# Deferring the outer layer norm of each token half in a fused attention, FFN and MoE kernel

## What is computed

```python
def _L0_attn_ref(src, ...):                      # x is src
    attn = _sliding_attn(qkv, qkv, qkv, W)       # 16 heads of 64, window 256
    x = _layernorm(src + attn, ln1_g, ln1_b)
    ff = jnp.maximum(x @ W1 + b1, 0.0) @ W2 + b2 # 1024 -> 4096 -> 1024
    return _layernorm(x + ff, ln2_g, ln2_b)
x = L0_attn_src
x = _layernorm(x + _L0_attn_ref(x, ...), axis=-1)   # the "outer" layer norm
x = _layernorm(x + _L0_ffn_ref(x, ...), axis=-1)    # MoE: 8 experts, top 2
```

## Time and profile before

| | |
|---|---|
| median of the runs | 3103.24 us |
| lowest to highest of 3 runs | 3102.35 to 3196.35 us |
| the profiled execution | 3100.56 us |
| its span on the slowest core (core 3) | 3099.4 us |
| spans of the 8 cores in it | 3088.9 to 3099.4 us |
| busy on that core: TensorE, VectorE, ScalarE, GpSimd | 74%, 26%, 16%, 16% |

### The profile page before, as it was taken

How to read it: one execution, slowest core, us unless ns; L and a number is a source line. 1 busy time by engine, 2 the same in 40 slices (tenths; PEclk the granted TensorE clock), 3 DMA queues, 4 the chain that set the end, 5 groups by cost and what they waited for, 6 DMA issues and landing times.

```text
span 3099.4 us, 31648 instructions; the slowest of 8 cores (3088.9 to 3099.4 us)
## 1 busy us (share of the span) xinstructions
PE 2301.0 (74%) x11290; PEld 1085.2 (35%) x11290; DVE 796.2 (26%) x1503; ACT 507.9 (16%) x751; POOL 509.8 (16%) x604
## 2 busy tenths in 40 slices
PE   0477877622999089922289988999889998999874
PEld 0243434311444034411134433444344443444431
DVE  0022222266000520053323311333113321233233
ACT  0233333300310022000011111111111111111110
POOL 2477777500000000000000001000100001000000
PEclk9999999999999599965589999999999999999987
DMA  9300000100442244302022223222332223222242
GB/s 217 72 1 1 1 1 1 36 5 0 69 81 55 55 68 81 68 8 47 1 48 41 48 48 69 34 41 41 62 62 35 48 41 62 55 37 46 48 102 75
DMA packets 49832, 148.18 MB, mean 48 GB/s; under 512 B 4952, under 2 KB 7680, under 8 KB 47632
## 3 DMA queue, kind: packets, MB, share of 16 engines
q0 software_dynamic: 41888, 123.88, 23.0%
q1 hardware_dynamic: 7792, 22.27, 2.3%
HBM read 248.96 MB, written 8.42 MB: 83 GB/s over the span
## 4 chain that ended last, share of the span: by engine, by line
PE 69%; DVE 11%; issue 5%; DMA 5%; ACT 4%; SPq 3%; POOL 3%; DVEq 0%; ACTq 0%; POOLq 0%
PE ob L670 14%; PE hg L605 14%; PE hu L605 14%; PE hb L477 7%; PE hb L448 6%; PE ppv L282 5%; DVE x0s L131 4%; PE ps L340 3%; SPq L154 3%; DVE bn L131 3%; POOL strb L145 3%; ACT osb L141 2%; DMA x0s<-x 2%; DVE attnh L134 1%; PE ptm L302 1%
## 5 line engine op out<-in xcount | busy, mean ns | idle before, releaser
L605 PE MATMUL hg<-ubf,w1T 128*128 128x512 bf16 x2048 | 486.7, 381 | 18.5 <-DMA w1T<-w1tt 9.5
L605 PE MATMUL hu<-ubf,w1T 128*128 128x512 bf16 x2048 | 483.8, 379 | 0.0
L670 PE MATMUL ob<-a,w2t 128*128 128x512 bf16 x2048 | 460.2, 384 | 10.3 <-DVE a L131 9.1
L145 POOL TENSOR_TENSOR strb<-strb,msk 128x640 bf16<-128x640 bf16 (+4 forms) x320 | 358.9, 1150 | 200.6 <-ACT strb L141 173.0
L131 DVE TENSOR_TENSOR x0s<-pbf,x0s 128x1024 f32<-128x1024 bf16 x80 | 98.0, 1225 | 949.2 <-PE pbf L688 493.2
L605 PEld LDWEIGHTS hg<-ubf,w1T 128*128 128x128 bf16 x2048 | 200.5, 98 | 262.7 <-issue 24.6
L448 PE MATMUL hb<-ybf,w1buf 128*128 128x512 bf16 x1024 | 228.4, 386 | 83.7 <-DMA w1buf<-W1p 78.2
L670 PEld LDWEIGHTS ob<-a,w2t 128*128 128x128 bf16 x2048 | 199.6, 99 | 244.6 <-issue 22.8
L605 PEld LDWEIGHTS hu<-ubf,w1T 128*128 128x128 bf16 x2048 | 200.5, 98 | 241.9 <-issue 0.7
L141 ACT ACTIVATE sg<-hg 128x512 bf16<-128x512 f32 x256 | 152.8, 597 | 743.4 <-PE hu L605 743.4
L131 DVE TENSOR_TENSOR sg<-sg,crep 128x512 bf16<-128x512 bf16 x256 | 108.9, 426 | 597.3 <-ACT sg L141 574.2
(11 more groups left out here) (64 smaller groups left out, 894.4 us busy)
## 6 DMA issues: line engine op xcount, KB each, us to landing
w1T<-w1tt POOLq DMA_DIRECT2D x64, 512.0 KB, 5.2
w2t<-w2tt POOLq DMA_DIRECT2D x128, 256.0 KB, 4.6
w1buf<-W1p POOLq DMA_DIRECT2D x32, 512.0 KB, 5.2
w2buf<-W2p POOLq DMA_DIRECT2D x16, 1024.0 KB, 8.5
x0s<-x SPq DMA_DIRECT2D x1, 8192.0 KB, 51.5
x0s<-x POOLq DMA_DIRECT2D x2, 4096.0 KB, 24.6
out<-x0s SPq DMA_DIRECT2D x2, 4096.0 KB, 14.2
x0tm<-x0p POOLq DMA_DIRECT2D x20, 260.0 KB, 39.7
```

Of the source, the lines that this page charges most:

```text
L145: getattr(self.nc.gpsimd, name)(*args, **kw).then_inc(self.sGP, 1)
L605: ins = nc.tensor.matmul(hps[:], bass.AP(self.w1T, slot2 * 2048 + kc * 256 + hu * 128, [[2 * 2048, 128], [1, 128]]), self.ubf[:, kc, 512 * ...
L670: ins = nc.tensor.matmul(obp[:, 512 * nb:512 * nb + 512], self.w2t[:, dsl, eidx, 128 * jc:128 * jc + 128], self.a[:, eidx, jc, 1024 * half ...
```

## The change

The inner layer norm of a half stays where it was. What follows it (the wait on GpSimd's queue, the accumulating load, VectorE's wait for it and the outer layer norm) becomes a function, `outer_ln_half`. For half 0 it is called within half 1, after the last group of FF1 and ahead of the first `W2` load. For half 1 it is called after the barrier and the set-up of the MoE buffers, ahead of the build of `ubf`. That build is called four times for 4 tiles each, with a wait for the outer layer norm of the half in question, where it was called once for 16 tiles.

```diff
@@ phase_ffn
         for half in range(2):
             ... # FF1: 16 groups
                 prev_w1_user[gslot] = self.cT
+            if half == 1:
+                self.outer_ln_half(0)
             for dc in range(FC):
                 ... # FF2
             self.waitd("vector", self.mg_tok)
-            ln2m = self.layernorm(gb=2, tiles=range(8 * half, 8 * half + 8))
-            self.wait("gpsimd", self.sV, ln2m)
-            xr = self.gdma(
-                self.x0s[:, 8 * half:8 * half + 8, :],
-                bass.AP(self.x0.tensor, (Q0 + 1024 * half) * D,
-                        [[D, 128], [128 * D, 8], [1, D]]),
-                accum=True)
-            self.waitd("vector", xr)
-            self.layernorm(gb=None, tiles=range(8 * half, 8 * half + 8))
+            self.ln2m[half] = self.layernorm(gb=2, tiles=range(8 * half, 8 * half + 8))
+
+    def outer_ln_half(self, half):
+        self.wait("gpsimd", self.sV, self.ln2m[half])
+        xr = self.gdma(
+            self.x0s[:, 8 * half:8 * half + 8, :],
+            bass.AP(self.x0.tensor, (Q0 + 1024 * half) * D,
+                    [[D, 128], [128 * D, 8], [1, D]]),
+            accum=True)
+        self.waitd("vector", xr)
+        self.u1m[half] = self.layernorm(gb=None, tiles=range(8 * half, 8 * half + 8))
@@ build, after the barrier that ends the FFN
-            self.m_ubf = self.fm_build(self.ubf, self.obs[0])
+            self.outer_ln_half(1)
+            ubf_q = {}
+            for qd in range(4):
+                ubf_q[qd] = self.fm_build(
+                    self.ubf, self.obs[0], tiles=range(4 * qd, 4 * qd + 4),
+                    dep=self.u1m[qd // 2])
+            self.m_ubf = ubf_q[3]
             self.phase_gating()
```

More of the change, by code:

```diff
@@ L428, in phase_ffn @@
         prev_w2_user = {}
+        self.ln2m = {}
+        self.u1m = {}
         mig_g = 0
```

## The result

The changed kernel takes 3052.05 us in the median; the kernel before, beside it, 3102.99. The ratio of the two is 0.983, with a 95% interval from 0.9818 to 0.9841, so about 53 us are gained (49 to 56). That is 1.7%, under the 2% that the prediction took as measurable, but the interval lies clear of 1. The forecast was 3046 us and a gain of 57.

A forecast was written before the change was run, and what follows sets the result against it. TensorE was taken as held between the FFN halves by GpSimd's queue, then ScalarE's. Terms -70.1 + 15.4 + 1.7 + 0.7 - 1.9 - 3.0 = -57.2 us against the median 3103.24 gave 3046 us, range 3041 to 3054.

The forecast's parts named there:

- (a): Gap between FFN halves: half 0's outer layer norm leaves it, gaining 70.1 us; an 11.7 us ReLU stall stays.
- (b): Start of half 1's FF2, t = 0 at the last `W1` issue: input load delays `W2`, 15.4 us lost, plus 1.7 low clock.
- R1: Rival at half 1's FF2: queue transfers share engines evenly, so `W2` is not held up; 3029 us, chance 0.10.
- The covers: In half 1's FF2, waits claimed free: first addition 0.5 us late, ScalarE's square root with 5 us to spare.
- (c): Half 1's outer layer norm behind the barrier: stays on the path; GpSimd's walk through the waits adds 0.7 us, 0 to 2.
- (d): Build of `ubf` in four calls: 1.9 us won at the first copy, 3.0 us at three seams.
- R4: Rival in the gap between halves: `W1` loads of half 1 still come late, 17 us lost; 3119 us, chance 0.02.
- R2: Rival in half 1: GpSimd's loads locked out during scaling, or input load some 10 us longer; 3056 to 3065 us, chance 0.12.
- the long form of R2: In half 1's FF1, GpSimd's loads locked out through the inner norm's whole scaling; a `W1` load 19 us late.
- the short form: In half 1's FF1, a `W1` load starts at most 0.81 us late per scaling instruction, with 1.7 us to spare.
- R3: Rival in half 1's matmuls: clock stays low after the stops; 3154 us for FF2, 3262 for the half; chance 0.03.

The follow-up runs named there:

- the repeat: The changed kernel run once more, with nothing altered, as the reference for later runs: 3047.8, 3049.7 and 3050.2 us, ratio 0.9827 to the kernel before.

## Why the prediction was right, step by step

The chain of steps was right, and so were nearly all sizes. Core 3 of both profiles, each step as a difference of two marks (the last flips of half 1 start at 1341.26 before and 1291.53 after):

| step | forecast | measured | how it is read |
|---|---|---|---|
| end of flips to the restart | -70.1 | -70.1 | 88.84 to 18.78 |
| restart to the last `W1` issue | 0 | +0.9 | 93.24 to 94.12 |
| last `W1` issue to FF2 | +15.4 | +15.9 | 18.49 to 34.34 |
| FF2's first matmul to the last flip | +1.7 | +1.7 | 126.65 to 128.37 |
| last flip to the input load's issue | +0.7 | +1.5 | 47.52 to 49.00 |
| issue to the end of the norm | 0 | +0.2 | 48.49 to 48.64 |
| norm to the first copy | -1.9 | -1.9 | 2.01 to 0.10 |
| first copy to gating | -3.0 | -3.7 | 65.94 to 62.20 |
| sum | -57.2 | -55.6 | |

Marks of the last four steps, the kernel before, then the changed one:

```profile
1388.78 1.60 POOL L164 DMA_DIRECT2D x0s<-x  x1 [79.64 <-DVE x0s L131]
...
1505.22 3.56 PE L522 MATMUL pf<-WgT,ubf 128*128 128x8 bf16 x128 [1.01 <-DVE ubf L131]
```
```profile
1340.53 1.60 POOL L164 DMA_DIRECT2D x0s<-x  x1 [81.10 <-issue]
...
1451.47 3.55 PE L528 MATMUL pf<-WgT,ubf 128*128 128x8 bf16 x128 [1.01 <-DVE ubf L131]
```

*(a)* The restart came 1034.70 - 1033.34 = 1.36 us after the square root, the figure taken over from before. What I had not got right is the low clock behind it. I had taken the restart to cost as much as before, at most 0.7 us more. It cost more: 58 matmuls took 15.48 us, 2.9 over the full rate of 0.218 each, where before 49 took 12.32, 1.6 over. That is 1.3 us more, and the +0.9 in the second row once small gaps that closed are taken off (a wait for `W1` in that stretch was 0.9 us before and is 0.6 now). The step is right; the bound of 0.7 on the low clock was too narrow by 0.6 us.

*(b)* Transfers landed in the queue's order: the input load landed at 1129.41 + 26.6 = 1156.0, which is t = 27.2 (27.4 to 30.2 forecast), and the first `W2` load at 1130.33 + 32.6 = 1162.9, t = 34.1 (33.9 forecast). The single terms were off against each other. The `W1` load pushed the input load by 2.1 us, less than the bound of 2.4, and the `W2` load came 6.9 us behind it, more than the bound of 5.8. That their sum came out within 0.2 us is luck. The idle time in the profile is 20.45 us and not 15.4 + 1.4, since FF1's last group ended earlier: it waited 0.52 us for its weights and not 2.08, and ran at the full clock, 3.2 us in all. Its load landed after 6.6 us with the input load behind it and after 8.1 with `W2` loads behind it, where 5.2 is usual: a load also takes longer for what stands behind it, so the transfers are not strictly one after another, as the prediction read the rows. I had counted from a load's issue to FF2, and by that the term holds. Moving the load (FF2 15.8 us earlier, counted from the last `W1` issue: 1147.38 - 1128.84 = 18.5) and halving it (the `W2` load 8.4 us sooner) show that this order, and for the most part the amount of bytes ahead, is the cause. R1, the even sharing of the queue, has fallen.

The covers held: FF2 itself took 1.7 us longer, the low clock's price, so the first addition and ScalarE's square root cost TensorE nothing.

*(c)* GpSimd's walk through the barrier cost 1.5 us and not 0.7, inside the 0 to 2. *(d)* A seam brought 3.7 / 3 = 1.2 us, not 1.0: VectorE waits 0.16 us for the second group where it waited 1.41.

The steps give 55.6 us and the times 53, with 56 as the interval's edge. Core 3 lies on the high side: from half 0's flips to gating the mean over the eight cores falls from 488.0 to 433.9 us, by 54.1 (52 to 58 by core; 433.6 in the repeat). Core 3's whole span fell by 47.7 only, as its last stage took 9.4 us longer in this execution. What remains of a difference is not settled; the spans of the cores also vary by some us from one execution to the next, and the slowest of eight counts.

Two of the recorded sums are off, without consequence: R4 comes to 3046 + 70.1 = 3116 us by its own terms, not 3119, and the second `W2` load's latest landing to t = 41.8, not 41.4.

R2, GpSimd kept from writing descriptors while VectorE scales, is the one for which the trace shows something. Core 3, timeline, the three `W1` loads in question:

```profile
1044.77 0.81 DVE L131 TENSOR_SCALAR x0s<-x0s,negm,inv 128x1024 f32<-128x1024 f32 x1
1045.17 0.53 POOL L164 DMA_DIRECT2D w1buf<-W1p  x1 [21.21 <-PE hb L450]
...
1051.93 0.81 DVE L131 TENSOR_SCALAR x0s<-x0s,negm,inv 128x1024 f32<-128x1024 f32 x1
1052.07 0.79 POOL L164 DMA_DIRECT2D w1buf<-W1p  x1 [6.38 <-PE hb L450]
...
1058.98 1.04 POOL L164 DMA_DIRECT2D w1buf<-W1p  x1 [6.12 <-PE hb L450]
1059.09 0.81 DVE L131 TENSOR_SCALAR x0s<-x0s,negm,inv 128x1024 f32<-128x1024 f32 x1
```

Each of the three issues ends 0.12 us after the end of the scaling that it met: 1045.70 after 1045.58, 1052.86 after 1052.74, 1060.02 after 1059.90. The first was due to end there anyway; the other two took 0.79 and 1.04 us where 0.53 is usual. The Trainium skill (SBUF — State Buffer, section "Who interferes with whom") says that VectorE in a two-port mode and GpSimd lock each other out of the ports that they share for a whole instruction, whoever comes first. For GpSimd's side the trace agrees: over all eight cores of this profile and of the repeat, each `W1` issue that began up to 0.54 us after the start of a scaling, or up to 0.11 us ahead of it, ended 0.12 us or more after that scaling. For VectorE's side it shows less: where the issue began 0.13 us or more ahead, it kept its 0.53 us, and the scaling that fell into it took at most 0.89 us, not 0.81. TensorE felt nothing of it: from 1034.70 on it first waits for `w1buf` at 1072, and then for 0.6 us. So the long form of R2 has fallen, and the short form costs nothing here, thanks to the 1.7 us to spare. R3 has fallen too: the extra 2.9 and 1.7 us after the two stops are what some 14 and 8 matmuls lose at half speed (0.21 us each, an estimate from these rows), so the clock was back within 16 matmuls. R4 has fallen with the first timeline.

## What to carry to other kernels

When work is taken out of a gap, read what it is put in front of: each engine's queue runs in program order, so the moved load delayed the next weights and the unmoved square root held up a ReLU, and reordering those two was worth another 32 us. A transfer that is beside matmuls is hidden only if nothing that the matmuls need soon stands behind it in the same queue; its price here was mostly the time of the bytes ahead, and with the next weights issued first core 3 had no stop left in half 1. A layer norm that crosses three engines has to be placed on each of them, not as one call.

## What was not expected

- TensorE's granted clock has been seen at a mean of 0.81, between its levels of 1.2 and 2.4 GHz, through long stretches in which it never paused. On core 1 it held through 60 us of matmuls (busy table, the same columns as above). On cores 2 and 3 the same came in the last stage: 32 matmuls took 8.57 us there, not 7.07. Each time it hit two cores of a pair together, and in the next profile of the same kernel it was gone from core 1's FF1, and core 3 had 1.00 over 20 us of that last stage. Its cause is open.

```profile
800.00:860.00 60.00, 60.00 (x230) 24.90 (x229) 0.00 (x0) 16.71 (x15) 3.70 (x7) 0.81 0.38 64
```

- How long the low clock lasts after a stop isn't given by the stop's length alone: after 5.44 us idle 49 matmuls cost 1.6 us extra, after 11.88 us 58 cost 2.9, after 20.45 us 64 cost 1.7, and after 4.74 us 64 cost 1.8. Nor is the cost fixed for one stop: the same 11.88 us on core 3 cost 1.6 us in the run with the `W2` loads first (384 matmuls in 84.52 us).
